# A decoder of thirteen blocks on one core: the next block's first rows normalised and turned ahead of ten block boundaries, and two sorted-expert blocks written out without loops

## The reference

```python
x = x + _L0_attn_ref(_layernorm(x), ...)            # an RWKV time mix and channel mix
x = x + _L0_xattn_ref(_layernorm(x), ctx, ctx, mask, ...)
x = x + _L0_ffn_ref(_layernorm(x), ...)             # ternary weights
x = x + _L1_attn_ref(...); x = x + _L1_xattn_ref(..., ctx, ctx, ...); x = x + _L1_ffn_ref(...)
x = x + _L2_attn_ref(...); x = x + _L2_xattn_ref(..., ctx, mask, 5); x = x + _L2_ffn_ref(...)
x = x + _L3_attn_ref(...); x = x + _L3_xattn_ref(..., ctx, ctx, deltas, mask, ...); x = x + _L3_ffn_ref(...)
```

## Time and profile before

| what | us |
|---|---|
| median of 3 runs (3132.84 to 3135.2) | 3135.05 |
| the profiled execution | 3131.25 |
| its span | 3129.5 |

### The profile page before, as it was taken

How to read it: one execution, slowest core, us unless ns; L and a number is a source line. 1 busy time by engine, 2 the same in 40 slices (tenths; PEclk the granted TensorE clock), 3 DMA queues, 4 the chain that set the end, 5 groups by cost and what they waited for, 6 DMA issues and landing times. The chain is left out here.

```text
span 3129.5 us, 46962 instructions
## 1 busy us (share of the span) xinstructions
PE 2637.7 (84%) x15124; PEld 1819.2 (58%) x15125; DVE 1832.2 (59%) x3997; ACT 1209.2 (39%) x3068; POOL 791.6 (25%) x613
## 2 busy tenths in 40 slices
PE   3998989899688785899989979869969687869996
PEld 1565766666455453677766757646645465446664
DVE  6884986488788445343444659843355588333334
ACT  2223654166677222344334436511212566212221
POOL 4433530144100132222222236421110233121110
PEclk8999999999787798999999999979989898989998
DMA  9001000000200323000000020140020300431113
GB/s 303 1 1 47 13 16 3 14 1 1 62 4 1 88 93 122 28 1 1 1 24 25 11 68 2 41 164 30 29 72 1 86 11 1 153 106 32 32 32 99
DMA packets 158960, 142.40 MB, mean 46 GB/s; under 512 B 59012, under 2 KB 146068, under 8 KB 158388
## 3 DMA queue, kind: packets, MB, share of 16 engines
q1 hardware_dynamic: 145828, 111.95, 12.5%
q0 software_dynamic: 8688, 23.82, 2.1%
q10 hardware_dynamic: 4256, 4.20, 0.4%
HBM read 97.12 MB, written 42.81 MB: 45 GB/s over the span
## 5 line engine op out<-in xcount | busy, mean ns | idle before, releaser
L873 POOL TENSOR_TENSOR room<-room 128x1024 f32<-128x1024 f32 x144 | 273.1, 1897 | 458.9 <-DVE room L818 458.6
L812 DVE TENSOR_REDUCE room<-room 128x8 f32<-128x1024 f32 x144 | 174.0, 1208 | 0.0
L1312 PE MATMUL l3f_hidden<-room,Y 128*128 x312 | 145.6, 610 | 1.2 <-DVE Y L1552 0.6
L1331 PE MATMUL l3f_out<-room,Y 128*128 x624 | 141.1, 379 | 1.6 <-DVE Y L1577 1.6
L549 PE MATMUL l2a_proj<-room 128*128 128x256 f32 x512 | 128.2, 399 | 14.3 <-ACT room L896 14.3
L1331 PEld LDWEIGHTS l3f_out<-room,Y 128*128 128x128 f32 x624 | 118.5, 190 | 34.1 <-issue 20.0
L873 POOL TENSOR_TENSOR room<-room,l2a_rinv 128x1024 f32<-128x1024 f32 x32 | 60.7, 1896 | 253.5 <-DVE l2a_rinv L818 253.5
L549 PEld LDWEIGHTS l2a_proj<-room 128*128 128x128 f32 x512 | 97.1, 197 | 32.0 <-issue 17.0
L1688 POOL DMA_INDIRECT results<-Y,l3f_dest x39 | 37.2, 955 | 296.6 <-DVE Y L1585 161.3
L942 ACT ACTIVATE room<-l2a_scores,l2a_nmx 128x128 f32<-128x128 f32 x256 | 72.3, 381 | 93.6 <-DVE l2a_nmx L804 93.6
L1659 ACT ACTIVATE Y<-l3f_hiddenT,vecs 128x128 f32<-128x128 f32 x156 | 44.6, 368 | 157.5 <-PE l3f_hiddenT L1322 157.5
(11 more groups left out here) (749 smaller groups left out, 6732.3 us busy)
## 6 DMA issues: line engine op xcount, KB each, us to landing
sorted_rows<-zeros SPq DMA_DIRECT2D x1, 16512.0 KB, 67.5
room<-in_L_ffn_w SPq DMA_DIRECT2D x16, 1024.0 KB, 12.4
room<-in_L_ffn_W SPq DMA_DIRECT2D x16, 1024.0 KB, 12.2
Y<-sorted_rows SPq DMA_DIRECT2D x62, 129.0 KB, 2.1
room<-in_ctx SPq DMA_DIRECT2D x24, 256.0 KB, 2.7
room<-results SPq DMA_DIRECT2D x12, 512.0 KB, 7.4
room<-sorted_rows SPq DMA_DIRECT2D x39, 129.0 KB, 2.1
Y<-results SPq DMA_DIRECT2D x8, 512.0 KB, 5.9
```

The costliest lines, as they stand in the source:

```text
L812: dve.tensor_reduce(rsum[:, u % 2, :], p[:, u % (TURN + 1), :, :], AX.X, ALU.add)
L873: pool.tensor_tensor(p[:, u % (TURN + 1), :, :], p[:, u % (TURN + 1), :, :], rinv[:, u % (TURN + 1), :].unsqueeze(2).to_broadcast([P, HEAD ...
L1312: mm = pe.matmul(hbank[a][:, :], rowsT[:, par, kc, :], chip.room[:, bass.ds(at + (kc * F + a * half_f), half_f)], start=(kc == 0), stop=(k ...
L1331: mm = pe.matmul(obank[par][:, 0:D], hT[:, f, :], chip.room[:, bass.ds(at + (SLOT // 2 + f * D), D)], start=(f == 0), stop=(f == HC - 1))
```

## The change

A class `Head` is added. At ten boundaries (from rwkv, l0x, l0f, l1a, l1x, l2a, l2x, l2fa, gau and l3x; not from l1f and l2fm) the block in front makes in its last steps the statistics of the next block's first four row blocks, normalises them into a buffer of its own that is no longer used, turns them by eight transposes into two PSUM banks and copies them, one half by DVE and one by ACT, to a new lasting buffer `chip.head` (which takes the place of `chip.zeros`). The next block takes its first group (or two pairs) from there. The statistics of all 16 blocks are now made in the next block: behind the opening in attention, first of all in the others; the end of the block in front has none. In attention POOL begins with the third pair, the opening of ctx blocks becomes q, c, m, k, v, and that of the others k, q, v. `begin_block` may also give a block's buffers spare room of the next block's arena. l1x aggregates each row block in its step and not all 16 at the end.

In `sorted_experts_block` the loops are written out, with waits on constants, and PE reads a tile's weight register once, ahead of its turn. The first group's normalising (still needed for the table) comes later, the next groups' between the router's steps; l2fm adds X + Y group by group, and its router loop has fewer stages. At l2fm's end ACT, not SP, issues gau's weights, ahead of the gathers, and l2fm leaves finished statistics.

```diff
+class Head:
+    def make_rows(self, dve, src):
+        ln_stats_vector(chip, dve, src, self.stats, chip.head_twice, have="mv", part=self.part)
+        for j in range(GR):
+            op = dve.tensor_scalar(self.rows[:, j, :], src[:, j, :], chip.mv[:, j, 0:1], scale[:, j:j + 1], ALU.subtract, ALU.mult)
+        op.then_inc(self.rows_ready, 1)
+    def roots(self, act):
+        ln_stats_scalar(self.chip, act, self.stats, self.chip.head_twice, part=self.part)
+    def turn(self, pe, banks):
+        pe.wait_ge(self.rows_ready, 1)
+        for kc in range(KC):
+            for j in range(GR):
+                mm = pe.transpose(banks[kc][:, j * P:(j + 1) * P], self.rows[:, j, kc * P:(kc + 1) * P], self.chip.ident[:, :])
+            mm.then_inc(self.turned, 1)
+    def copy_first(self, dve, bank):
+        dve.wait_ge(self.turned, 1)
...
+            dve.tensor_copy(self.chip.head[:, 0, :], bank[:, :])
+    def copy_second(self, act, bank):
+        act.wait_ge(self.turned, KC)
...
+            act.copy(self.chip.head[:, 1, :], bank[:, :])
```

```diff
@@ attention_block @@
-    if ctxsrc:
+    if ctxsrc and chip.has_head:
+        opening = qs + [("c", 0)] + ([("m", 0)] if plan.mask == "support" else []) + ks + vs
+    elif ctxsrc:
         opening = [("c", 0)] + ([("m", 0)] if plan.mask == "support" else []) + ks + vs + [("y", 0)] + qs
     else:
-        opening = steady
+        opening = steady[1:] if chip.has_head else steady
...
+                    if t == T + 1 and head:
+                        pe.wait_ge(exps_done, 2 * T)
+                        head.turn(pe, scores)
...
-                ln_stats_vector(chip, dve, chip.X, s, plan.double_ln, have=have_stats)
-                dve.sem_inc(stats_ready, 1)
+                if not chip.has_head:
+                    statistics()
...
+                if chip.has_head:
+                    statistics()
...
+                    if t == T and head:
+                        dve.drain()
+                        head.make_rows(dve, resid)
+                    if t == T + 2 and head:
+                        head.copy_first(dve, scores[0])
                 dve.drain()
-                ln_stats_vector(chip, dve, resid, end, leave_twice, have="mv")
+                if not head:
+                    ln_stats_vector(chip, dve, resid, end, leave_twice, have="mv")
...
-                next_rows(0)
+                if first_turned:
+                    next_rows(first_turned)
+                else:
+                    next_rows(0)
...
+                    if t == T and head:
+                        head.roots(act)
+                    if t == T + 2 and head:
+                        head.copy_second(act, scores[1])
```

```diff
@@ sorted_experts_block @@
-                    for k in range(NG + 3):
+                    for k in range(NG + 1):
+                        if first_turned <= k < NG:
+                            turn_rows(k)
                         if k < NG:
-                            turn_rows(k)
-                        if 0 <= k - 1 < NG:
-                            logits_flat(k - 1)
-                        if 0 <= k - 2 < NG:
-                            logits_back(k - 2)
-                        if 0 <= k - 3 < NG:
-                            rank(k - 3)
+                            logits_flat(k)
+                        if k:
+                            rank(k - 1)
+                        if k < NG:
+                            logits_back(k)
...
-                with pe.Fori(0, NT // 2) as i:
-                    step(i, 0)
-                    step(i, 1)
-                turn_hidden(NT // 2, 0)
-                second_layer(NT // 2, 0)
+                for n in range(NT):
+                    after = None
+                    if n + 1 < NT:
+                        after = weights_of(n + 1)
+                        turn(n + 1)
+                    turn_hidden(n)
+                    if n + 1 < NT:
+                        first_layer(n + 1, after)
+                    second_layer(n, at)
+                    at = after
...
-                if prefetch:
-                    prefetch.load(sp)
+                if prefetch:
+                    act.preload_act_table(ACT.Sqrt)
+                    act.wait_ge(out_filled, NT)
+                    prefetch.load(act)
+                    ln_stats_scalar(chip, act, final)
...
-LEAVES_STATS = {**{b: "rstd" for b in PLANS}, "rwkv": "rstd", "l1x": "rstd", "l1f": "rstd", "l2fm": "bn", "l0f": "rstd", "gau": "rstd"}
+LEAVES_STATS = {**{b: "mv" for b in PLANS}, **{b: "mv" for b in ("rwkv", "l0f", "l1x", "gau")}, "l1f": "rstd", "l2fm": "rstd"}
+LEAVES_HEAD = ("rwkv", "l0x", "l0f", "l1a", "l1x", "l2a", "l2x", "l2fa", "gau", "l3x")
```

579 lines of the change are left out of this document (346 added, 233 removed).

## The result

The changed kernel took **3117.82 us** (median of 5 runs, 3115.25 to 3118.85), the kernel before 3135.05 (3132.84 to 3136.28): the ratio is 0.9945, 95% interval 0.9933 to 0.9957, so 17.2 us less. I had forecast 39 less, 3096, with a range of 3062 to 3122. The sign is right and the time lies in the full range, but the size is less than half of the forecast, and the narrower range of the forecast itself, 3080 to 3112, is missed.

What follows compares the result with a forecast made beforehand. PE was busy for 84% of the span, so time was to be gained where it stands still, at block boundaries. A +13.6, B -11.6, C -35.6 and D -4.8 sum to -38.4: 3096 us, full range 3062 to 3122.

Steps and rivals of the forecast that it cites:

- rival 1: Tails at ten boundaries: A's whole chain lies on the path, +40 in place of +13.6, 3122 us; chance 0.13.
- A: Work put into the old block's last steps at ten boundaries: +13.6 us, of it +3.0 in l1x.
- B: Closing statistics leave the blocks' ends: -11.6 us, of it -1.0 for l1x's 16 aggregates moved into its steps.
- C: The next blocks' openings, which find their first rows turned: -35.6 us, statistics made after the opening included.
- Rival 3: Nothing gained: openings wait for what the change does not touch; within 3129 to 3141 us; chance 0.05.
- The rule against it: l1a's and l2fa's openings: POOL's passes block DVE's L717 through the shared ports, 2 x 2.4 us more, 3101; nothing charged.
- l1f: -1.0 (statistics instead of four normalising passes): l1f's opening: 1.0 us saved, as statistics replace four normalising passes.
- rival 2: PE's gaps become short enough that the clock stays up: at most 24.7 us more back, 3071; chance 0.17.
- D: The rest (straight expert loops, second pair's y turn, l2fm to gau): -4.8 us, loops -1.4 in l3f and -0.9 in l2fm.
- gau's weights, now issued ahead of the gathers, compete with them: -0.5, ends -2 and +3: l2fm to gau: statistics move ahead of the barrier while weights compete with gathers; -0.5 us, between -2 and +3.
- l2fm: -2.1 taken, near the middle: l2fm's opening: router loses its first turn but its groups go one behind the other; -2.1 us, bounds -9 and +3.
- Rival 4: Slower: the expert tiles' straight code must be fetched, 62 us for 62 tiles, 3158 us; chance 0.07.

Runs made afterwards that it cites:

- e3: The changed kernel with eight unused transposes of the identity added on PE at l1f's start: 3107.8 us, ratio 0.99.
- e4: The changed kernel without the head that l1x leaves to l1f, which turns its first group itself: 3108.97 us, ratio 0.9909.
- e15: The kernel before, unchanged, profiled a second time in a single execution: 3133.69 us.
- e12: The kernel before with the changed expert block alone (loops written out, router's order, l2fm's end), no heads: 3141.99 us, ratio 1.0017.
- e16: The kernel before with 2000 drains each of ACT and POOL at l3f's end, a single execution: 3245.53 us, drains included.
- e1: The changed kernel measured again without edit: 3120.33 us, ratio 0.9943.
- e2: The changed kernel with gau's weights issued by SP behind the gathers, as before: 3112.16 us, ratio 0.9924.
- e8: The changed kernel without any head; closing statistics come back and those of the opening stay: 3156.39 us, ratio 1.0065.
- e18: The kernel of e17 with all 16 aggregates in l1x's steps, each behind its own drain: 3097.65 us, ratio 0.9891.
- e5: The changed kernel with e2's and e3's edits together: 3102.26 us, ratio 0.9887.
- e7: e5 with l1x's root ahead of ACT's casts and twelve of its aggregates at the end again: 3100.16 us, ratio 0.9885.
- e11: e7 without l1x's head and without the unused transposes in l1f: 3093.0 us, ratio 0.9869.
- e13: e7 with the groups of l2fm's router overlapped again, DVE normalising two groups ahead: 3100.2 us, ratio 0.9882.
- e14: The kernel of e11 with l2fm's router overlapped as in e13: 3095.96 us, ratio 0.9875.
- e17: The kernel of e11 measured again, unchanged: 3099.01 us, ratio 0.9885.
- e9: e7 with eight unused transposes of the identity for each group of l2fm's router: 3103.81 us, ratio 0.9886.

## Why the prediction was half right

The sum comes to 3096.65. The measured 3117.82 lies inside the full range by luck: its upper part, 3112 to 3122, was there for rival 1, the tails, and these cost what was forecast. What brought the time there was something else, above all the clock in l1f and the weights at l2fm's end.

**A, the tails: right.** Summed over the ten boundaries, the last steps grew by 13.9 us against 13.6 forecast (l0x 1.7, l1a 0.6, l1x 4.1, l2fa 1.9, gau 2.1, l3x 1.3, the others 0.25 to 0.9), measured in the first two profiles as the shift of the block's last work against its steps. Single terms were off by up to 1.4. Rival 1 (+40) is out.

**B and C, statistics and openings: right in sum in the blocks that hold nothing else.** l1a -6.4 against -6.0, l0x -2.4 against -3.6, l3x -3.6 against -4.0, l3f -6.5 against -5.4. l2x gave 4 more and l2fa 4.6 less: by the shift of the first steps l2x's opening gave 7.8 where I took 3.5, and l2fa's 2.8 where I took 5.5. That these two cancel is luck. So, in part, is l3x, whose time varies by 10 us with the same code. Rival 3 (nothing gained) is out by l1a alone.

The traces show where l2fa's 2.8 comes from, as far as this goes without an experiment. Its first scores come some 7 to 8 us earlier, but the half clock, which had lain over the opening, now lies behind it. The second pair's projections (L549, now L614), in the timeline of PE, before and after:
```profile
1866.89 1.99 PE L549 MATMUL l2fa_proj<-room 128*128 128x256 f32 x8
```
```profile
1856.75 3.59 PE L614 MATMUL l2fa_proj<-head,room 128*128 128x256 f32 x8
```
In l2x the half clock fell from some 13 us to 3.4 in both pairs of profiles, and its opening gave more than I took.

The rule against it (DVE's L717, now L790, blocked by POOL's passes) did not come to a test: POOL's first pass in l1a starts at 619.16, behind the statistics, when L790 (611.88 to 615.59) is done.

**C, "l1f: -1.0 (statistics instead of four normalising passes)": failed.** The term counted DVE's work and left out what the eight transposes did for PE. They were the uninterrupted work in which the clock rose; without them it stayed at 1.2 GHz and the shared layer came 4.7 later (e3 and e4 give it back). My rival 2 had the clock rise everywhere as gaps shrink. It did so in l1a and l2x (at the half clock for 14 us each, then for 3 to 7), but the reverse in l1f (69 and 70 us, then 91 and 78) and l2fm; over the whole span the half clock went from 503.6 and 506.4 us to 511.6 and 522.1. The rest of l1f's +7.9 is mostly the wait that e15 shows in the kernel before: the three profiles with l1f's old code and the wait (e12, e15, e16) have 217.8 on the mean, the changed kernel, e1 and e2 222.1, which is 4.3 more.

**D, "gau's weights, now issued ahead of the gathers, compete with them: -0.5, ends -2 and +3": failed.** It measured +5.85, outside its ends, and e2 takes 5.33 of it away. The step named the competing transfer but set it against the gathers alone, which lost some 1.5; it left out POOL's last send, on whose landing SP stands with all gathers queued behind, and this lost 3.9.

**C, "l2fm: -2.1 taken, near the middle": off.** The first tile comes 50.94 and 51.60 us after the block's start, before 51.41 and 49.97: 0.6 later on the mean, within the bounds of -9 and +3, and one of the signs that I had named for being wrong. e12 and e8 (55.98 and 55.71 without a head) show two large parts that cancel: the head gives some 4 to 5, and the router as rewritten costs 4.6 to 6.0.

**B, "In l1x 16 aggregates leave the end for slack in the steps (-1.0)", and A's +3.0: off.** The q bias is 2.8 earlier to the tenth, and the first distances even 4.9, in both pairs of profiles. But the steps gave some 4 of it back and the tail took 4.1. What the steps lost it to is open: e18's 2.05 for the aggregates would be half of it, if it is theirs.

**D, the loops: right.** In the first two profiles the tiles took 1.0 less in l2fm and 1.4 less in l3f, against 0.9 and 1.4. Rival 4 (code fetching) is out: no tile got longer.

With the weights and l1f's clock mended (e5, e7, e11, e13, e14, e17, e18) the kernel lies 32 to 44 us below the kernel before, where 39 were forecast. So a gain of the size that I summed can be had, and the miss is mostly what the change does beside it. That the sum fits does not prove each term: l2x, l2fa and l1x are off by 4 each, four of these kernels have one head less, and some of the difference between them is l3x's 10 us.

## What to carry to other kernels

Taking work away from TensorE ahead of a stretch of many small matmuls can lengthen that stretch: look at the granted clock behind the place, not only at the gap. Filling the gap is no rule either: in l2fm's router the same unused transposes cost 3.1 us (e9). A prefetch that is moved forward to an idle engine's queue can hold up a small transfer on whose landing others wait: look for that transfer first. It was the larger part of the loss here. And profile the kernel before twice ahead of building on one wait: here a wait of 5 to 12 us was missing from the first profile alone.

## What the runs showed of the hardware that I had not expected

- Eight transposes that nobody reads made l1f some 5 us shorter (shared layer after 25.72 us instead of 30.77), with the clock at 1.00 instead of 0.50 in the second 10.2 us stretch.
- A shorter gap does not make the half clock go, it can move it: in l2fa's second 10 us eight equal projections took 3.59 us where they had taken 1.99, although PE's first gap in that block had shrunk from 10.14 us to 2.26.
- A DVE operation on 128x16 elements, 0.17 us elsewhere, took 3.50 us beside POOL's memset of 3.51 in l1x. Both operands lie in SBUF. The Trainium skill, "SBUF — State Buffer", in the list of terms, has the pair of ports that DVE and GpSimd share as an exclusive lock held for the whole instruction; the trace agrees here.
- In l1f, while POOL scatters, DVE stands still some 1 us at a time before instructions that wait for nothing the profile shows. PE's wait ahead of the matmul shown above was 5.3 to 12.4 us in 19 profiles and 3.21 in one; the cause is open.
